# Stacks read by few transfers with a repeated source row, rows ordered by dimension, and each part written on its own

## The reference, cut to what matters

```python
# attention a, x is the normed input
q, k, v = (proj(w_q), proj(w_k), proj(w_v))       # 16 heads of 16 dimensions
sq, sk = elu1(q), elu1(k)
out_m = einsum('bhsd,mhde->mbhse', sq, memories) / clip(rel, EPS)[..., None]
mem_out = einsum('mbhse,mbh->bhse', out_m, softmax(rel.mean(-1), axis=0))
num = sq . cumsum(sk x v);  den = sq . cumsum(sk)  # causal
out = g * mem_out + (1 - g) * num / den            # then @ w_o.T
...
# attention b
scores = einsum('bhqd,bhkd->bhqk', rope(q), rope(k)) * scale
attn = softmax(where(causal, scores, -inf));  out = attn @ v   # then W_O
```

## Time and profile before

| | |
|---|---|
| median of 3 runs | 2301.34 us |
| profiled execution, its span | 2303.04 us, 2301.3 us |
| TensorE busy | 1904.0 us, 83% |
| vector, scalar, GpSimd busy | 1617.6, 1361.3, 1140.6 us |
| granted TensorE clock, mean | 0.936 |
| transfers, mean rate | 126.64 MB, 55 GB/s |

### The profile page before, as it was taken

The page is one execution under the profiler, slowest core; times in us unless marked ns, Lnnn a source line. Parts: engine busy times, 40 slices in busy tenths (PEclk is TensorE's granted clock), DMA queues, the critical chain, the costliest instruction groups (busy, mean ns, idle before and its releaser), DMA issues. The chain is left out here.

```text
span 2301.3 us, 53268 instructions
## 1 busy us (share of the span) xinstructions
PE 1904.0 (83%) x18306; PEld 1207.5 (52%) x18306; DVE 1617.6 (70%) x3890; ACT 1361.3 (59%) x2694; POOL 1140.6 (50%) x978
## 2 busy tenths in 40 slices
PE   0447798989899898989889898989889898988786
PEld 0224455655555555555555555655555555555443
DVE  5546686968777786968777786968777786966351
ACT  0215375666667575666667575666667575665554
POOL 0236347364655547364655547364655547363322
PEclk9757799999999999999999999999999999999998
DMA  3101312304031322303032221304032221303020
GB/s 104 55 10 55 65 57 47 84 5 99 30 70 60 66 66 47 84 9 95 29 70 61 66 66 47 84 2 102 30 65 66 66 66 47 84 2 66 9 58 10
DMA packets 101756, 126.64 MB, mean 55 GB/s; under 512 B 19760, under 2 KB 88496, under 8 KB 97456
## 3 DMA queue, kind: packets, MB, share of 16 engines
q1 hardware_dynamic: 93104, 115.10, 19.8%
q10 hardware_dynamic: 8448, 8.39, 1.1%
HBM read 80.95 MB, written 42.47 MB: 54 GB/s over the span
## 5 line engine op out<-in xcount | busy, mean ns | idle before, releaser
L1268 DVE TENSOR_REDUCE mxs<-bank 128x1 f32<-128x128 f32 (+3 forms) x1024 | 428.0, 482 | 79.7 <-PE bank L1561 78.8
L907 ACT ACTIVATE place<-bank 128x512 f32<-128x512 f32 (+1 forms) x768 | 349.7, 532 | 104.4 <-PE bank L1575 103.1
L669 POOL TENSOR_TENSOR place<-am,place 128x512 f16<-128x512 f32 x256 | 291.0, 1157 | 203.2 <-ACT place L813 203.2
L659 POOL TENSOR_TENSOR place<-place 128x512 f16<-128x512 f32 x256 | 300.7, 1182 | 69.6 <-ACT place L801 64.0
L1559 PE MATMUL bank<-kst,qst 96*128 96x128 f16 (+3 forms) x1024 | 250.8, 306 | 33.5 <-DVE mxs L1268 16.9
L1420 PE MATMUL bank<-w2q,place 128*128 128x256 f16 x2048 | 248.2, 274 | 5.8 <-ACT place L798 4.2
L644 POOL TENSOR_TENSOR rstd<-ve,halfc 128x4 f32<-128x4 f32 x64 | 64.8, 1012 | 364.6 <-DVE ve L1043 364.6
L1573 PE MATMUL bank<-qst,kst 128*128 128x512 f16 (+3 forms) x1024 | 230.7, 302 | 14.6 <-DVE mxs L1268 6.5
L697 POOL TENSOR_TENSOR place<-place 128x512 f16<-128x512 f32 x64 | 83.1, 1301 | 280.9 <-ACT place L837 259.8
L1561 PE MATMUL bank<-mask_qk,identb 128*128 128x128 bf16 x1024 | 218.2, 222 | 0.0
L1420 PEld LDWEIGHTS bank<-w2q,place 128*128 128x128 f16 x2048 | 195.3, 98 | 40.8 <-ACT place L798 11.7
(11 more groups left out here) (162 smaller groups left out, 4134.9 us busy)
## 6 DMA issues: line engine op xcount, KB each, us to landing
by_head<-place SPq DMA_DIRECT2D x64, 256.0 KB, 2.3
qst<-by_head SPq DMA_DIRECT2D x256, 64.0 KB, 2.3
kst<-by_head SPq DMA_DIRECT2D x256, 64.0 KB, 2.3
by_dim<-place SPq DMA_DIRECT2D x64, 256.0 KB, 2.5
kst<-by_dim SPq DMA_DIRECT2D x64, 256.0 KB, 4.7
qst<-by_dim SPq DMA_DIRECT2D x128, 128.0 KB, 5.5
xa<-x SPq DMA_DIRECT2D x16, 512.0 KB, 4.0
out<-xg ACTq DMA_DIRECT2D x16, 512.0 KB, 3.4
```

The costliest lines, as they stand in the source:

```text
L659: G.tensor_tensor(L.hl[:, m, :], L.hf[:, m % 2, :], L.hh[:, m, :], ALU.subtract).then_inc(s["hl"], 1)
L669: G.tensor_tensor(alp[:, n % 2, k, :], am[:, k, :], ahp[:, n % 2, k, :], ALU.subtract).then_inc(s["al"], 1)
L907: A.activation(pf[h % SLOTS][:, S2_COL[k]:S2_COL[k] + S2_W[k]], bank_of(L2, ("S2", h, k))[:, 0:S2_W[k]], ACT.Exp, scale=D ** -0.5 / RS ** ...
L1268: V.tensor_reduce(mxs[:, g:g + 1], bank_of(L2, ("S1", n, k))[:, Q_AT[i]:Q_AT[i] + (i + 1) * P], AX, ALU.max).then_inc(s["mx"], 1)
```

## The change

Four things, in one edit:

- The weights of attention a's q and k are stored so that lane 1's projected rows are ordered by group of four heads, then dimension, then head in the group (`split_by_dim`). The memories, the block mask (`bd4` in place of `bd8`) and the slices in `outputs` follow. The order for lane 2 stays and is written by other instructions (`split_by_parity`).
- DRAM: `by_head` becomes `by_row`, in which a row of 4 KB holds four heads one behind the other.
- Writes: each of the four parts of a half (q high, q low, k high, k low) is written by its own transfer of 128 KB once it is there, instead of two transfers once all are.
- Reads: a source of which the rows are repeated by a leading dimension with step 0 (`broadcast_to([2, ...])`) replaces reads that were issued once for each copy. Lane 2 has three a half (512, 256, 256 KB), and lane 1 six (two of 256 KB, four of 128 KB).

```diff
-OUTS = dict(v=2, vh=2, sh=4, sl=4, bounced=64, wo=2, xres=2)
+OUTS = dict(v=2, vh=2, sh=4, sl=4, bounced=128, wo=2, xres=2)
-LANDED = {1: 2 * 4 * 2 * 16, 2: 6 * 16}
+LANDED = {1: 6 * 16, 2: 3 * 16}
...
-        by_head = nc.dram_tensor("by_head", (KH, 2, P, 2, S), F16, kind="Internal").ap()
+        by_row = nc.dram_tensor("by_row", (KH, 2, 2, 2, PARTS, S), F16, kind="Internal").ap()
...
-        DVE_SETUP = 66
+        DVE_SETUP = 75
...
-                sp.wait_ge(s["sh"], due(L, "sh", t, 2 * half + 2))
-                sp.wait_ge(s["sl"], due(L, "sl", t, 2 * half + 2))
-                for part, src in enumerate((L.sth, L.stl)):
-                    to = by_head[half, part] if L is L1 else by_dim[half, :, part].rearrange("w p s -> p w s")
-                    sp.dma_start(to, src[:, 2 * half:2 * half + 2, :]).then_inc(s["bounced"], 16)
-
-                sp.wait_ge(s["bounced"], due(L, "bounced", t, 32 * (half + 1)))
+                for which in range(2):
+                    row = 2 * half + which
+                    for part, (name, src) in enumerate((("sh", L.sth), ("sl", L.stl))):
+                        sp.wait_ge(s[name], due(L, name, t, row + 1))
+                        to = by_row[half, which, :, part] if L is L1 else by_dim[half, which, part]
+                        sp.dma_start(to, src[:, row, :]).then_inc(s["bounced"], 16)
+
+                sp.wait_ge(s["bounced"], due(L, "bounced", t, 64 * (half + 1)))
...
-                    for k in range(2):
-                        sp.dma_start(L.kst[2 * k * D:2 * (k + 1) * D, heads, :].rearrange("p h s -> p (h s)"),
-                                     by_dim[half, 1].rearrange("a (d h) s -> (a d) (h s)", h=HH8)
-                                     ).then_inc(L.landed[half], 16)
-                        for j in range(2):
-                            row = (2 * k + j) * D
-                            sp.dma_start(L.qst[row:row + D, heads, :].rearrange("p h s -> p (h s)"),
-                                         by_dim[half, 0, k].rearrange("(d h) s -> d (h s)", h=HH8)
-                                         ).then_inc(L.landed[half], 16)
+                    k_rows = by_dim[half, 1].rearrange("a (d h) s -> (a d) (h s)", h=HH8)
+                    sp.dma_start(L.kst[0:PARTS, heads, :].rearrange("p h s -> p (h s)"),
+                                 k_rows.rearrange("(o r) f -> o r f", o=1).broadcast_to([2, 2 * D, HH8 * S])
+                                 ).then_inc(L.landed[half], 16)
+                    for part in range(2):
+                        q_rows = by_dim[half, 0, part].rearrange("(o d h) s -> o d (h s)", o=1, h=HH8)
+                        sp.dma_start(L.qst[2 * part * D:2 * (part + 1) * D, heads, :].rearrange("p h s -> p (h s)"),
+                                     q_rows.broadcast_to([2, D, HH8 * S])).then_inc(L.landed[half], 16)
                     return
-                for k, (q_part, k_part) in enumerate(((0, 0), (0, 1), (1, 0), (1, 1))):
-                    for dst, part, which in ((L.qst, q_part, 0), (L.kst, k_part, 1)):
-                        rows = by_head[half, part, :, which, :]
-                        for r in range(2):
-                            to = slice(r * PARTS + k * D, r * PARTS + (k + 1) * D)
-                            sp.dma_start(dst[to, pairs, :], rows.rearrange("(g r d) s -> r d g s", r=2, d=D)[r]
-                                         ).then_inc(L.landed[half], 16)
+                for r in range(2):
+                    k_rows = by_row[half, 1, r].rearrange("a (d h) s -> (a d) (h s)", h=QH)
+                    sp.dma_start(L.kst[r * PARTS:(r + 1) * PARTS, pairs, :].rearrange("p h s -> p (h s)"),
+                                 k_rows.rearrange("(o r) f -> o r f", o=1).broadcast_to([2, 2 * D, QH * S])
+                                 ).then_inc(L.landed[half], 16)
+                    for part in range(2):
+                        q_rows = by_row[half, 0, r, part].rearrange("(o d h) s -> o d (h s)", o=1, h=QH)
+                        row = r * PARTS + 2 * part * D
+                        sp.dma_start(L.qst[row:row + 2 * D, pairs, :].rearrange("p h s -> p (h s)"),
+                                     q_rows.broadcast_to([2, D, QH * S])).then_inc(L.landed[half], 16)
...
+            def split_by_dim(mat):
+                stage = w_stage[mat // BQ][:, 0:2 * KH * H].rearrange("p (j i d) -> p j d i", i=QH, d=D)
+                hi, lo = (both(w, mat).rearrange("p (j d i) -> p j d i", i=QH, d=D) for w in (wh, wl))
+                for i in range(QH):
+                    link(V.tensor_scalar(hi[:, :, :, i], stage[:, :, :, i], WS, None, ALU.mult))
+                    link(V.scalar_tensor_tensor(lo[:, :, :, i], stage[:, :, :, i], WS, hi[:, :, :, i],
+                                                ALU.mult, ALU.subtract))
...
-            split_weights(0, BQ)
+            split_by_dim(AQ)
+            split_weights(AV, BQ - AV)
             split_by_parity(BQ)
-            split_by_parity(BK)
             split_weights(BV, NMAT - BV)
...
+            link(V.tensor_reduce(bd4, ident[:, :].rearrange("p (j i) -> p i j", i=QH), AX, ALU.add))
...
-                        ins = T.matmul(local[r][:, i], part[:, n % 2, h % 2, (h // 2) * P:(h // 2 + 1) * P],
+                        ins = T.matmul(local[r][:, i], part[:, n % 2, r, i * P:(i + 1) * P],
```

More of the change, by code:

```diff
@@ L440, in build @@
         coef = sb("coef", [P, 2, 2, TERMS, QH])
-        bd8 = am[:, 0, 0:HH8]
+        bd4 = am[:, 0, 0:QH]
         t6 = L1.place3[:, 0:3, :].rearrange("p a s -> p (a s)").rearrange("p (r t s) -> p r t s", r=2, t=M + 2)
@@ L519, in _ @@
                 for h in range(HH8):
-                    sp.dma_start(bm[h * D:(h + 1) * D, half, :, h % QH, :], mem[half * HH8 + h]).then_inc(m_in, 16)
+                    r, i = divmod(h, QH)
+                    sp.dma_start(bm[r * PARTS + i:(r + 1) * PARTS:QH, half, :, i, :],
+                                 mem[half * HH8 + h]).then_inc(m_in, 16)
             sp.wait_ge(primed, 1)
@@ L610, in _ @@
             G.memset(mask_kq[:, :], 0.0).then_inc(pool_const, 1)
-            G.memset(bd8, 1.0).then_inc(pool_const, 1)
             G.memset(nt[:, :, :], 0.0).then_inc(pool_const, 1)
             G.memset(halfc[:, :], -0.5).then_inc(pool_const, 1)
-            pool.wait_ge(pool_const, 8)
+            pool.wait_ge(pool_const, 7)
             G.affine_select(out=ident[:, :], in_=ident[:, :], compare_op=ALU.not_equal, fill=1.0, base=0,
@@ L623, in _ @@
                             pattern=[[1, P]], channel_multiplier=-1).then_inc(pool_const, 1)
[L625 to L629, removed]
             pool.wait_ge(c_in, 96)
-            pool.wait_ge(pool_const, 14)
+            pool.wait_ge(pool_const, 11)
             for L in (L1, L2, F2, F1):
@@ L968, in split_weights, with both @@
                 link(V.scalar_tensor_tensor(lo, stage, WS, hi, ALU.mult, ALU.subtract))
-            def split_by_parity(mat):
[L971 to L980, removed]
-            split_weights(0, BQ)
+            def both(tile, mat):
+                return tile[:, mat:mat + 2, :, :].rearrange("p n k f -> p (n k f)")
+            def split_by_dim(mat):
[5 more added lines that the diff above has]
+                                                ALU.mult, ALU.subtract))
+            def split_by_parity(mat):
+                stage = w_stage[mat // BQ][:, 0:2 * KH * H].rearrange("p (j h m r) -> p r m j h", r=2, m=D // 2, h=HH8)
+                hi, lo = (both(w, mat).rearrange("p (j r m h) -> p r m j h", r=2, m=D // 2, h=HH8) for w in (wh, wl))
+                for r in range(2):
+                    for m in range(D // 2):
+                        link(V.tensor_scalar(hi[:, r, m], stage[:, r, m], WS, None, ALU.mult))
+                        link(V.scalar_tensor_tensor(lo[:, r, m], stage[:, r, m], WS, hi[:, r, m], ALU.mult, ALU.subtract))
+            split_by_dim(AQ)
+            split_weights(AV, BQ - AV)
             split_by_parity(BQ)
-            split_by_parity(BK)
             split_weights(BV, NMAT - BV)
@@ L1006, in _ @@
                 link(V.scalar_tensor_tensor(w, stage, small[:, 4 + n:5 + n], below, ALU.is_gt, ALU.subtract))
-            dve.wait_ge(pool_const, 14)
+            dve.wait_ge(pool_const, 11)
             link(V.tensor_copy(identh[:, :], ident[:, :]))
+            link(V.tensor_reduce(bd4, ident[:, :].rearrange("p (j i) -> p i j", i=QH), AX, ALU.add))
             link(V.tensor_copy(identb[:, :], ident[:, :]))
@@ L1026, in _ @@
                                    bm[rows, :, :, :, D].rearrange("p a m h -> p (a m) h")))
-                link(V.tensor_copy(bdmask[rows, :, :], bd8[rows, heads].rearrange("p (h o) -> p h o", o=1)
+                link(V.tensor_copy(bdmask[rows, :, :], bd4[rows, :].rearrange("p (h o) -> p h o", o=1)
                                    .broadcast_to([PARTS, QH, VW])))
```

## The result

The changed kernel takes 3555.0 us, the median of four runs (3551.04 to 3558.1), beside 2301.48 us for the one before (four runs, 2298.95 to 2302.83). The ratio is 1.5445, with a 95% interval of 1.5426 to 1.5465: 1254 us slower.

A forecast was written before the change was run, and what follows sets the result against it. TensorE, busy 1904 us of 2301.3, was taken as the bound. 14 turns at +70.6, two at +37, two at +30 and +2 setup made 1124 us: 3425 us on the median, range 2850 to 3950.

The forecast's parts named there:

- the forecast's own case: Two engines carry each repeated read, a half's reads taking 21.7 to 34.7 us: 3023 to 3855 us, chance 75 in 100.
- What bounds the kernel, and the cover of each read set: TensorE bounds; 10 us lie between issue and use of lane 2's first stacks, 14 us for lane 1's first half.
- Two of 16 engines for each repeated read: Stack reads with leading dimension 2 are each carried by two of 16 DMA engines.
- The same two each time: All repeated reads use the same two DMA engines, so the read sets queue behind one another.
- T = 28: Duration in us of one half's stack reads on two DMA engines, one value for both lanes, between 21.7 and 34.7.
- A turn: One loop turn with both lanes: 4T + 88.4, 200.4 us at T = 28, 70.6 more than 129.8.
- stage 3: Lane 1's half 0: 13.1 us to its first write, write to reads 2.8, the reads, 1 to land; 44.9 us.
- stage 4: Lane 1's half 1: 2.5 us, the reads, then 1 with the last `mrow` behind them; 31.5 us.
- The clock: TensorE's clock drops after each of four stops a turn; 4 us added behind the second and fourth, 8 a turn.
- Setup +2: Vector engine's setup chain has nine instructions more, 75 for 66, some 0.2 us each: +2 us.
- TensorE's own instructions 0: TensorE runs the same matmuls with other slices: 0 us.
- Earlier writes 0: Writing each part when ready: at most 14 us, less than 0.5 us of each half here, counted as 0.

The follow-up runs named there:

- e1: The changed kernel with each copy of a stack's rows read by its own transfer, without repeated source; lane 1's writes as in the change: 2501.5 us, ratio 1.0858.
- e4: The changed kernel with the q reads of each set issued ahead of the k reads: 3540.76 us.
- e7: e6 with eight 0.06 us instructions added to the vector engine's setup, 66 in all as in the kernel before: 2296.28 us, ratio 0.9969.
- e2: e1 with each lane 1 write also cut in two along its leading dimension, eight of 64 KB a half: 2329.82 us, ratio 1.0121.
- e10: e7, but the sync engine waits for all four parts of a half before the first write, as before the change: 2304.2 us, ratio 1.0012.
- e3: e2 with only lane 2's reads repeated, as in the change: 2874.93 us.
- e8: e2 with only lane 1's reads repeated, as in the change: 2741.95 us.
- e9: The changed kernel with lane 1's writes cut as in e2, all repeated reads kept: 3287.64 us.
- e5: The kernel before with nine 0.06 us memsets added to the vector engine's setup, 75 instructions for 66: 2325.51 us, ratio 1.0098.
- e6: e2 with fewer instructions for the high parts of the split matrices, 58 and not 75 in the vector engine's setup chain: 2336.94 us, ratio 1.0146.

## Why the prediction was right

It gave 3425 us; 3555 was measured, 130 more, inside the range of the forecast's own case. The mechanism was the forecast's; that the number came so near is in part luck, since errors of its terms cancelled. Its steps, one by one:

- *What bounds the kernel, and the cover of each read set*: right. The largest waits stand in the places named, and no other engine became the bound.
- *Two of 16 engines for each repeated read*: right, by the packets (2 small ones a read), the share (0.13) and e1, which takes the repeat away and gains 1054 us. The rule of the Trainium skill ("DMA: Bandwidth & Descriptors", why a DMA increments its semaphore by 16) agrees with all three. *The same two each time*: the share stays at 0.13 where a set's reads are all under way, so they share them.
- *T = 28*: 30.0 us at most and 28.3 in lane 2 (1792.64 to TensorE's start at 1822.59, and 1825.22 to 1853.5), 24.5 and 23.9 in lane 1 (1884.46 to 1909.0, 1919.31 to 1943.2), where 1853.5 and 1943.2 are the ends of the stretches at a share of 0.13, and 1822.59 and 1909.0 TensorE's starts, so that the first value of each lane holds the landing too. The prediction took one value for both. In lane 2 the k read is slow, as it assumed (for a reason that no run shows), but at 31 to 33 GB/s for the two engines, not at 22, and the q reads move 53, not 48.
- *A turn*: the stages, in the order of the prediction, with T = 28, and what was measured between the rows above.

| stage | forecast | measured |
|---|---|---|
| 1. first write to head 0 | 31.9 | 34.3 |
| 2. half 1 of lane 2 | 31.5 | 31.9 |
| 3. half 0 of lane 1 | 44.9 | 54.6 |
| 4. half 1 of lane 1 | 31.5 | 35.2 |
| 5. to the next first write | 52.6 | 53.2 |
| clock, all stages | 8 | in the stages |
| sum | 200.4 | 209.1 |

The term that was mis-sized is "write to reads 2.8" in stage 3: it measured 15.5, since lane 1's writes are confined as well. That is 12.7 us too little. The same in stage 4: 10.3 us from the head of the third group (1909.00) to the reads (1919.31), where the forecast had 2.5, 7.8 too little. The row for it was at hand: the new write's shape `[2, 64, S]` follows from the shape of `by_row` in the diff, and the argument of the earlier trace rows holds for it word for word. These 20.5 us were in part made up for: lane 1's shorter T gives 8.6 back, and the clock some 6. With 2.8 more in stages 1 and 2 the turn was forecast 8.7 us short, 122 us over 14 turns, which is nearly all of the 130.
- *The clock*: 0.50 in each stop and 0.80 over the turn. Its 8 us were too many. Behind stop 2 the clock was at 0.50 over 1854 to 1858 and at 0.97 over the next 4 us, and the 13.1 us to lane 1's first write took 14.5; behind stop 4 it was at 0.62 over 1944 to 1948, and stage 5 took 53.2 for 52.6. That is 2 us for 8.
- *Setup +2*: +4.1. The first normalisation starts at 70.36 where it was 66.23. Of this 0.3 is a later arrival of the weights, which varies (in e1 to e4, with the same chain, the splits began between 20.2 and 23.7). A pair on 256 columns took 0.45 and 0.73 us, four of them 4.7. The estimate scaled from contiguous columns; these read and write with a stride. In e7 one such instruction over 1024 columns with the stride (L984) took 1.04 us and a contiguous one (L975) 0.69, so the stride costs time by itself.
- *TensorE's own instructions 0*: right for their number. *What is ahead of the loop costs nothing beyond its own time*: this was tacit and wrong. Of the 28 us of e2, 24.6 lie between lane 2's first write of sequence 0 and that of sequence 15, where the stops are (1948.7 us for 1924.0). The rest is setup and the ends of the run, less what early writes give.
- *Earlier writes 0*: not tested in this kernel. With all transfers spread they are worth 8 us (e7 and e10), out of the 14 named as the most, and nearly all ahead of the loop.

The account of the 1254 us by runs: setup and the loop's place 28 (e2), lane 2's repeated reads 545 (e3), lane 1's 412 (e8), lane 1's writes 267 (from e9 to the changed kernel); 1252. The split depends on the order: the writes alone cost 172. With ends included, a read set of lane 2 costs 17.0 us of the whole time for each of its 32 halves, and one of lane 1 12.9.

## What to carry to other kernels

Look at the leading dimension of both sides of every transfer, writes too: the number of small packets in the page and the DMA share of a stretch in which it runs alone tell how many of 16 engines carry it. Fewer transfers with a repeated row lost 958 us here (e9 less e2) against one transfer a copy that moves the same bytes. And when a program with a loop moves by one or two per cent after a change in its setup, compare the instruction queue's packets and the waits on "issue" at the loop's first instruction before looking for a cause in the loop.

## What the runs showed of the hardware that was not expected

- The place of a loop in an engine's instruction stream is worth 2.6 to 2.9 us at each jump back, here 23 us for nine instructions of 0.06 us more (e5), and 40.7 us for eight of them in the other direction (e6, e7). In which positions it appears was not mapped: 58 and 75 instructions ahead have it, 66 don't.
- Two DMA engines moved 53 GB/s together in the q reads, 26.5 each, more than the 24.1 of the earlier trace rows with all 16, and 31 to 33 in lane 2's k reads, of which the copies go to partitions 0 to 31 and 32 to 63, wherever in the set they stood (e4). Lane 1's k reads into partitions 64 to 127 ran at 52.
- A transfer of 512 KB over 128 partitions that was issued behind such a set (`xa<-x`) landed after 22.2 us at the median, against 4.0 before, and the issue of four writes behind a set held the sync engine for 14.2 and 15.5 us (1801.81, 1895.77): what stands behind a confined set is late as a whole.
